# A fused linear-attention and mixture-of-experts kernel: z in three fp32r matmuls, attention values of all batches computed during routing, 14 batches ahead of the experts, one more instruction per tile sent

## What is computed

```python
xn = layernorm(x)
# attention: 16 heads of 8 columns, 32 features per head
q, k, v = split(xn @ w_qkv)
q1 = exp(q @ proj - max(q @ proj));  k1 = exp(k @ proj - max(k @ proj))   # the max over the 32 features of a head
kv = k1^T v;  k_sum = sum of k1 over the tokens
att = (q1 kv) / (q1 k_sum + 1e-6) @ w_out + b_out
# experts: 8 of them, two per token
scores = (xn @ router_w^T + router_b) / max(temperature, 0.1)
gates = sinkhorn(scores)          # 3 times: minus logsumexp over experts, minus logsumexp over 128 tokens
top 2 gates, made to sum to 1
expert = (relu(xn wg) * (xn wp)) wo, weighted by the two gates, added to xn
```

## Time and profile before

| what | us |
|---|---|
| median of 3 runs | 333.81 |
| lowest and highest of them | 331.07 and 334.24 |
| the profiled execution | 333.39 |
| its span, first to last instruction | 331.3 |
| TensorE busy in the span | 289.8 (87%) |
| VectorE busy | 249.8 (75%) |
| GpSimd busy | 203.3 (61%) |
| ScalarE busy | 141.8 (43%) |

### The profile page before, as it was taken

One profiled execution on the slowest core, in us unless ns is written; L12 is line 12 of the kernel. 1 busy time (PEld: TensorE's weight loads), 2 busy tenths in 40 slices (PEclk: granted clock), 3 DMA queues, 4 the chain that ended last, 5 costly groups with the idle time before them and its releaser, 6 DMA issues.

```text
span 331.3 us, 6734 instructions
## 1 busy us (share of the span) xinstructions
PE 289.8 (87%) x1988; PEld 248.3 (75%) x1988; DVE 249.8 (75%) x619; ACT 141.8 (43%) x297; POOL 203.3 (61%) x303
## 2 busy tenths in 40 slices
PE   4996858899999999999996999999999999999300
PEld 4894336677777777887776999999999999779200
DVE  4866788856787777777775899999999997772283
ACT  3494432033444455554543555555555554452000
POOL 4000000188888788888500388888888888888391
PEclk9999585659999999999996999999999999999755
DMA  7974000011211111219220488888878871111793
GB/s 239 349 259 147 1 2 16 1 53 61 71 60 69 51 69 60 69 61 309 81 67 0 118 250 237 250 244 258 253 240 248 253 208 49 40 48 49 221 406 134
DMA packets 33749, 46.43 MB, mean 140 GB/s; under 512 B 5472, under 2 KB 22368, under 8 KB 33728
## 3 DMA queue, kind: packets, MB, share of 16 engines
q1 hardware_dynamic: 28608, 36.19, 35.6%
q0 software_dynamic: 4544, 9.84, 8.4%
q10 hardware_dynamic: 576, 0.15, 0.2%
HBM read 27.17 MB, written 17.68 MB: 135 GB/s over the span
## 4 chain that ended last, share of the span: by engine, by line
PE 70%; DVE 10%; POOL 7%; DMA 5%; issue 3%; ACT 1%; SPq 1%; DVEq 0%; POOLq 0%
PE bank L533 14%; PE bank L704 10%; PE bank L554 6%; PE bank L578 6%; PE bank L692 5%; PE bank L693 5%; PE bank L694 5%; POOL rows_y L457 4%; PE bank L568 3%; PE bank L487 3%; DMA x_tile<-slots_x 3%; PE bank L677 3%; PE bank L504 2%; PE bank L540 2%; DVE acc L987 2%
## 5 line engine op out<-in xcount | busy, mean ns | idle before, releaser
L449 POOL DMA_INDIRECT slots_x<-xn,slot_i x64 | 63.3, 989 | 70.8 <-DVE slot_i L1088 60.0
L457 POOL DMA_INDIRECT rows_y<-xn,row_i x78 | 80.6, 1034 | 38.6 <-DVE xn L1175 25.4
L776 ACT ACTIVATE feat<-z_sb 128x512 f32<-128x512 f32 x64 | 39.9, 631 | 72.2 <-DVE z_sb L943 72.1
L936 DVE TENSOR_REDUCE neg_max<-bank 128x16 f32<-128x512 f32 x64 | 43.8, 686 | 28.4 <-PE bank L533 28.4
L692 PE MATMUL bank<-xT_high,w_high 128*128 128x256 f32 x156 | 48.2, 309 | 1.2 <-DVE w_low L1183 1.2
L693 PE MATMUL bank<-xT_low,w_high 128*128 128x256 f32 x156 | 45.0, 288 | 0.0
L694 PE MATMUL bank<-xT_high,w_low 128*128 128x256 f32 x156 | 44.7, 286 | 0.0
L943 DVE TENSOR_TENSOR z_sb<-bank,neg_max 128x512 f32<-128x512 f32 x64 | 42.5, 682 | 1.4
L704 PE MATMUL bank<-w_tile,hidden 128*128 128x128 f32 x312 | 41.3, 275 | 0.0
L533 PE MATMUL bank<-w_feat,xT_stage 128*128 128x512 f32 x80 | 40.1, 603 | 0.0
L704 PEld LDWEIGHTS bank<-w_tile,hidden 128*128 128x128 f32 x312 | 38.2, 192 | 0.1
(11 more groups left out here) (140 smaller groups left out, 489.2 us busy)
## 6 DMA issues: line engine op xcount, KB each, us to landing
w_tile<-w_expert_dram SPq DMA_DIRECT2D x39, 384.0 KB, 3.7
slots_x<-zeros SPq DMA_DIRECT2D x39, 144.0 KB, 2.3
x_tile<-slots_x SPq DMA_DIRECT2D x39, 130.0 KB, 3.3
acc<-x_dram SPq DMA_DIRECT2D x8, 256.0 KB, 5.5
xn<-rows_y SPq DMA_DIRECT2D x8, 256.0 KB, 5.6
w_tile<-rows_y SPq DMA_DIRECT2D x8, 256.0 KB, 5.8
out_dram<-acc SPq DMA_DIRECT2D x8, 256.0 KB, 3.4
xT_stage<-xnT SPq DMA_DIRECT2D x10, 128.0 KB, 2.0
```

What stands on the lines that cost most here:

```text
L449: pool.indirect_dma_start(slots_x, bass.IndirectOffsetOnAxis(slot_i[k][:, i:i + 1], 0), xn[:, j, :], None).then_inc(scattered[n % FLIGHT], 16)
L457: pool.indirect_dma_start(rows_y, bass.IndirectOffsetOnAxis(row_i[:, k, t:t + 1], 0), y_tile(k, t), None)\
L776: act.activation(feat[par][n][:, :], z_sb[n][:, :], ACT.Exp).then_inc(feat_ready, 1)
L936: dve.tensor_reduce(neg_max[n][:, :], args(n), AX_X, ALU.max, negate=True).then_inc(z_negmax, 1)
```

## The change

- **z in fp32r.** `xnT` and `w_feat` are each split in a high and a low fp32r part, and each `z` is three fp32r matmuls 128 x 512 in place of one fp32 matmul. The weights are split by VectorE, `xnT` by GpSimd (a cast and a subtraction of 128 x 512 for each of eight groups, after the layer norm).
- **Values during routing.** `v` and `copy_v` are gone from the steps; `values(g)` (TensorE, four matmuls 128 x 128) and `copy_values(g)` (ScalarE, 128 x 512) do each of the eight groups of tiles within the routing links. `v_aug` holds `xnT` until then; GpSimd sets its columns of ones (`set_ones`).
- **Early stages.** GpSimd, not VectorE, normalises two tiles of each group. `feature_weights` stands before the groups, the last `router` before the first z. Warm-up is 8 `keep_warm` at the start and 2 for each group.
- **Routing.** The bias of the router is scaled once, so that the scores need one VectorE operation. The sum of the gates moves to GpSimd (three additions and one more) and the division to `share`; `choose` works on `gate_exp`. `mask` is in order of experts, so that `place` scans it out of PSUM and needs fewer operations; the two counting matmuls are in fp32r. `mask_kv(0)` stands after the mask.
- **EARLY is 14**: steps 1 to 13 stand before the experts, batches 14 and 15 after them. The loop is unrolled and SyncE's `stage` is gone. GpSimd scatters 5 rows tiles per step (PER_TWO = 10), the last when `z_shifted` reaches 57, the first z of step 13.
- **Start of the experts.** The first two weight splits stand before step 13 on ScalarE and VectorE (`first_weights_high`, `first_weights_low`); `keep_warm(6)` and `keep_warm(4)` stand around the first transposes.
- **Sending.** After each of the 39 tiles GpSimd does one memset of 128 x 1 (`gap`).
- **The end.** GpSimd adds both planes of groups 0 to 3 to `acc`, VectorE those of groups 4 to 7; VectorE's last division and projection stand between its groups, and `denominators(15)` behind its first group. SyncE stores four groups, ScalarE four.

```diff
-    EARLY = 13
+    EARLY = 14
-    PER_BATCH = 6
-    LEAD = 6
+    PER_TWO = 10
+    LEAD = 1
...
-            with engine.Fori(LOOP_FROM // 2, EARLY // 2) as i:
-                step(2 * i, i, 0)
-                step(2 * i + 1, i, 1)
-            for b in range(EARLY // 2 * 2, EARLY):
+            for b in range(1, EARLY):
+                if b == EARLY - 1 and ahead_of_last:
+                    ahead_of_last()
                 step(b, b // 2, b % 2)
...
+        def combine(engine, k, g, added, before):
+
+            engine.wait_ge(plane_landed[k][g], 16)
+            if k == 1:
+                engine.wait_ge(added, TOPK * before + 1)
+            tiles = acc[:, g * GROUP:(g + 1) * GROUP, :].rearrange("p j d -> p (j d)")
+            engine.tensor_tensor(tiles, y_plane(k, g), tiles, ALU.add).then_inc(added, 1)
...
+            for g in range(NG):
+                cols = slice(g * GROUP * P, (g + 1) * GROUP * P)
+                pool.wait_ge(xnT_copied, g + 1)
+                pool.tensor_copy(by_token_tile(xnT_high[:, cols]), xnT_group(g)).then_inc(xnT_rounded, 1)
+                pool.wait_ge(xnT_rounded, g + 1)
+                pool.tensor_tensor(by_token_tile(xnT_low[:, cols]), xnT_group(g), by_token_tile(xnT_high[:, cols].bitcast(F32)),
+                                   ALU.subtract)\
+                    .then_inc(xnT_split, 1)
...
-                    pool.wait_ge(z_shifted, 4 * LOOP_FROM - LEAD + 4 * n // PER_BATCH)
+                    pool.wait_ge(z_shifted, 4 * LOOP_FROM - LEAD + 8 * n // PER_TWO)
...
                     for piece in range(n * NT // SLOT_TILES, (n + 1) * NT // SLOT_TILES):
                         add_bias(piece)
+                pool.memset(gap[:, k:k + 1], 0.0)
...
-                pe.matmul(bank[Z_BANK + n][:, :], xT(f, par, n % 2), w_feat[:, n // 2, :],
-                          start=True, stop=True).then_inc(z_ready, 1)
...
+                pe.matmul(to, xT(xnT_high, f, half), w_feat_high[:, qk, :], start=True, stop=False)
+                pe.matmul(to, xT(xnT_high, f, half), w_feat_low[:, qk, :], start=False, stop=False)
+                pe.matmul(to, xT(xnT_low, f, half), w_feat_high[:, qk, :], start=False, stop=True).then_inc(z_ready, 1)
+
+            def values(g):
+                if g == 0:
+                    pe.wait_ge(weights_landed, 16 * N_WEIGHTS)
+                if g >= 2:
+                    pe.wait_ge(v_copied, g - 1)
+                for t in range(GROUP):
+                    mm = pe.matmul(v_bank(g)[:, t * P:(t + 1) * P], xnT(g * GROUP + t), wv_sb[:, :], start=True, stop=True)
                 mm.then_inc(v_ready, 1)
...
-            pe.wait_ge(v_copied, EARLY + 1)
             pe.wait_ge(z_shifted, 4 * (EARLY + 1))
             pe.wait_ge(acc_added, EARLY - 1)
-            pe.wait_ge(att_ready, EARLY)
+            keep_warm(6, 4)
             rows_T(0, 0, 0)
             rows_T(1, 0, 1)
+            keep_warm(4, 4)
             up(0, 0, 0)
+            pe.wait_ge(att_ready, EARLY)
...
+            for b in range(EARLY, NB):
+                step(b, b // 2, b % 2, front=b + 1 < NB)
+            dve.wait_ge(bias_added, 2 * NT)
+            combine_group(0)
+            denominators(NB - 1)
+            invert(NB - 1)
+            divide(NB - 1)
+            combine_group(1)
+            combine_group(2)
+            add_projection(NB - 1)
+            combine_group(3)
```

380 lines of the change are left out of this document (203 added, 177 removed).

## The result

| | before | after |
|---|---|---|
| median of the runs, us | 333.81 (331.07 to 334.24, 5 runs) | 324.07 (322.99 to 324.30, 5 runs) |
| ratio, 95% interval | | 0.9714 [0.9676, 0.9752] |
| span of the profiled execution, us | 331.3 | 322.1 |
| first send, last send (start), us | 186.8, 304.7 | 174.7, 296.0 |

The changed kernel is 2.9% faster, 9.7 us by the medians and 9.2 by the two spans. The forecast was 324.9.

A forecast was written before the change was run, and what follows sets the result against it. TensorE was taken to bound early attention, GpSimd's sends the end from the first send on. 333.4 - 3.2 - 0.9 - 5.1 - 1.7 + 3.2 - 1.2 = 324.5, plus 0.4 for the median: 324.9 us, range 317 to 331.5.

The forecast's parts named there:

- Term 1: Routing, up to the denominators of batch 0: VectorE's path gets shorter, a gain of 3.2 us.
- I take 3.2: Routing: the gain chosen between bounds of 1.5 and 5, after savings summing to 4.3 us.
- the better case: Rival, chance 0.22: full clock in routing, memsets cost 0.03 us, row tiles arrive in time; 320.2 us.
- Term 2: Step 1 of early attention: four z and one v change, partly at the lower clock; gain 0.9 us.
- Term 3: Early attention, steps 2 to 13: twelve steps of 7.66 us instead of eleven of 8.95, less split delay; gain 5.1 us.
- Term 4: Last denominators to first send: earlier start and higher clock, less row tiles about 0.9 late; gain 1.7 us.
- Term 5: GpSimd's sends: 32 memsets behind a bias piece at 0.10 us each; a loss of 3.2 us.
- my bound from below: Sends: each of the 39 memsets delays the next instruction by only 0.03 us, 1.2 us in all.
- Term 6: The end: VectorE needn't wait for GpSimd's last addition, but has four more small operations; gain 1.2 us.
- The step stays longer: Rival, chance 0.12: in early attention kv waits for divide and scatters set the pace, steps of 8.2; 331.4 us.
- the case in which reads exclude each other: Rival, chance 0.12: GpSimd and VectorE block each other, a final pair takes 1.95 us, routing loses some 2; 329.2 us.
- The slower case: Rival, chance 0.06: each memset between sends costs 0.6 us by draining the engine, 23.4 instead of 3.2; 345 us.

The follow-up runs named there:

- b2: Changed kernel without the 39 memsets and with the bias pieces between sends replaced by eight GpSimd additions during routing: 308.55 us.
- a1: Changed kernel without the 39 memsets between the sends: 320.75 us, ratio 0.9645.
- a3: Changed kernel with the first two weight splits of ScalarE and VectorE back behind step 13: 321.36 us, ratio 0.9659.
- a4: Changed kernel with each z as one fp32 matmul on the high parts instead of three fp32r matmuls: 331.26 us, ratio 0.9976.
- c2: Changed kernel without the ten small matmuls ahead of the first expert products, on a chip where the kernel before took 363.56 us: 329.89 us, ratio 0.9090.
- b1: Kernel before, with four small extra matmuls ahead of each row and column wait of the routing links: 330.39 us, ratio 0.9888.
- b3: Changed kernel with eight bias additions during routing, no memsets, 13 early batches, and first weight splits behind step 13: 301.52 us, ratio 0.9058.
- d2: Changed kernel without the ten small matmuls ahead of the first expert products, rerun beside a kernel before of 333.7 us: 322.48 us, ratio 0.9669.

## Why the forecast came true, and where it didn't

**What bounds the kernel.** The statement that the sends set the end from the first one on held in every run that touched it: without memsets the time fell by what the sends lost, with a later or earlier first send it moved with it, and a batch moved into the tail cost nothing. It also has its limit: without bias pieces the chain left GpSimd (b2).

**Term 1** (forecast -3.2, measured -6.6) has one part of the right size and two that are not. The links of the changed kernel begin and end here on VectorE's timeline (first row maximum, first top):

```profile
25.73 0.42 DVE L1080 TENSOR_REDUCE row_max<-scores 128x32 f32<-128x256 f32 x1
...
45.75 0.42 DVE L1059 TENSOR_REDUCE top<-gate_exp 128x32 f32<-128x256 f32 x1 [0.35 <-ACT gate_exp L863]
```

| part of term 1 | forecast | measured | from |
|---|---|---|---|
| up to the first row maximum | -1.0 | -3.4 | 29.08, 25.73 |
| the links, to the gates | +1.1 | +0.3 | 19.75, 20.02 |
| the gates' sum and division | -1.5 | -1.5 | 1.51, 0 |
| first top to denominators of batch 0 | -1.8 | -2.0 | 15.08, 13.07 |

The largest part of the miss lies ahead of the links. The scores operation and the z_max gave the 1.0 that I had for them. The other 2.3 are the early stages, for which my sum has no term at all: ScalarE's copy of the last transposed group starts at 23.34 instead of 25.46. It is also the least steady part. In the other profiles with the changed early stages this copy starts between 22.4 and 25.6, so the new lists and the luck of one execution can't be told apart here.

The +1.1 is the step "I take 3.2" out of 4.3: the value matmuls and GpSimd's splitting in the way, and the clock left low; the clock stood only in the better case, at -1.8. In this profile neither side won: the clock was down (0.69) from 29 to 34 us, where the kernel before had 0.97, and up from 34 to 42, where it had 0.59. One of VectorE's operations took 1.04 us instead of 0.42 beside GpSimd's last split. In a1, a3, a4 and c2, with the clock at 1.00 from 29 to 48, the same links take 18.5 us: 1.2 less than before, and 0.8 more than b1 at the same clock, which has neither value matmuls nor splits in them. So the clock is worth 2.0 us in the links of the kernel before (b1), and the changed kernel keeps some 1.2 of it when it has the clock throughout. It didn't in the execution that the ledger is from. I had argued against the clock with the ten us from 48 to 58, which lie behind the links and stayed low (0.67 after); the links themselves, at 0.59 from 34 to 42 before, I hadn't looked at.

**Term 2** (-0.9, -2.2) has its size in this one profile only. In other profiles with the same step it took 9.4 (b3 and c2, granted clock 0.82) to 12.1 us (b2, 0.58), against 11.68 (0.71) before: it goes by where the clock rises, and in most of them little of the gain is left.

**Term 3** (-5.1, -0.3) is the one that failed most. Two sizes were off, both with the right mechanism. An fp32r matmul of 512 columns starts 0.23 and not 0.215 after the one before it, so a z costs 0.70 and not 0.645; that makes steps of 7.85 instead of 7.66, and 12 x 0.19 = 2.3 us. The value came from halving an fp32 instruction; the doubled 256-column distance, my upper bound (0.24), was nearer. The other is the weight splits: "delay its divide, +1.4" counted VectorE's two instructions and not that the first waits for ScalarE's high parts (1.21), nor what the pause does to the next step (9.41). a3 puts them at 3.9, +2.5. Together 4.8, the whole miss. The first size is steady (7.85 in every profile at full clock); the second would be +0.9 in an execution whose last step has the full clock, as in a1. The bound was right: TensorE without a gap, kv and scatters never in its way.

**Term 4** (-1.7, -3.0). The earlier start is as forecast: the first product came 2.52 us after the last denominators (168.92 - 166.40) instead of 3.38. From there to the first send 5.8 instead of 7.9, by the clock (1.00, before 0.70), forecast 1.8. What I had set against it, row tiles 0.9 late, didn't show: TensorE's small matmuls stood where it would have waited 0.58 for the first tile (d2). c2 and d2 refute the reason I gave in part: the small matmuls aren't what holds the clock.

**Term 5** (+3.2, +3.4) has the right size by a wrong step. "32 memsets behind a piece at 0.10" is 31 at 0.03, which was my bound from below; the other 2.6 us are bias pieces that fell on VectorE's weight splits (a1), which I hadn't in the sum.

**Term 6** held its sign only: the end gave 0.5 of 1.2. Beside each other the additions take 1.53 to 1.71 on GpSimd and 1.20 to 1.57 on VectorE, which is seen here:

```profile
306.78 1.70 POOL L311 TENSOR_TENSOR acc<-w_tile,acc 128x512 f32<-128x512 f32 x1
...
307.45 1.57 DVE L311 TENSOR_TENSOR acc<-w_tile,acc 128x512 f32<-128x512 f32 x1
```

GpSimd's additions start 1.71 us apart ((313.62 - 306.78) / 4), less than the 1.26 + 0.69 = 1.95 of an addition of each alone. The Trainium skill (SBUF — State Buffer, Who interferes with whom) has a VectorE instruction with two inputs in SBUF and a GpSimd instruction that reads SBUF shut each other out for a whole instruction; by that a pair would take 1.95, an estimate. The trace agrees that they slow each other, not that nothing overlaps.

**The rivals.** The better case had the memset's 0.03 right for the usual piece, and the rows cost nothing as the kernel stands. Its clock in the links is seen in b1 and in some variants, and only in part in the changed kernel's own profile. "The step stays longer" had a wrong mechanism, kv and the scatters, and 6.5 us where the steps missed 4.8; the steps are longer, but by the fp32r rate and the splits. Of the case in which reads exclude each other, the pieces and the operations beside a split or an addition show the hold-up, the end shows less than the full 1.95, and the time didn't follow. The slower case, a memset at 0.6, fell: 0.09 us each, all told. So the forecast of the time was right partly by luck: errors of +4.8 and -6.0 met, and several of them go by where the clock falls in the one execution that was profiled.
